# Eight of the sixteen difference chunks of a batch built by TensorE, and three hand-overs rewritten, in a two-layer graph kernel

## The reference

```python
def L0(x, adj, W, b, a):                      # 4 heads of 32 channels
    h = (x @ W + b).reshape(Bb, Nn, H, D)
    e = e_i[:, :, None, :] + e_j[:, None, :, :]         # e_i, e_j: h times the two halves of a
    e = where(adj > 0, where(e > 0, e, 0.2 * e), NEG)
    return einsum('bijh,bjhd->bihd', softmax(e, axis=2), h)

def L1(x, adj, W1, b1, g1, be1, W2, b2, Wg, ...):
    D = abs(x[:, :, None, :] - x[:, None, :, :])        # 32 x 256 x 256 x 128
    h = einsum('bijc,oc->bijo', D, W1) + b1             # 64 channels out
    m, v = mean(h, (0, 1, 2)), mean((h - m) ** 2, (0, 1, 2))
    h = leaky((h - m) / sqrt(v + EPS) * g1 + be1)
    A = softmax(where(adj > 0, h @ W2.T + b2, NEG), axis=-1)
    ...                                                 # y from A and x, normalised; [x, y] @ Wt.T + bt
x = layernorm(x + L0(x, adj, ...)); x = layernorm(x + L1(x, adj, ...))
```

## Time and profile before

| | us |
|---|---|
| median of 3 runs | 2476.84 |
| lowest, highest | 2466.27, 2483.92 |
| profiled execution | 2493.66 (span 2491.8) |

### The profile page before, as it was taken

How to read it: one execution, slowest core, us unless ns; L and a number is a source line. 1 busy time by engine, 2 the same in 40 slices (tenths; PEclk the granted TensorE clock), 3 DMA queues, 4 the chain that set the end, 5 groups by cost and what they waited for, 6 DMA issues and landing times.

```text
span 2491.8 us, 35885 instructions
## 1 busy us (share of the span) xinstructions
PE 2032.6 (82%) x12869; PEld 822.0 (33%) x12869; DVE 2112.6 (85%) x2600; ACT 2252.3 (90%) x3500; POOL 53.7 (2%) x50
## 2 busy tenths in 40 slices
PE   5777766888888888888888888887888888888876
PEld 3555542323333323233323232232222222222225
DVE  4888866999999999999999999999878888788866
ACT  4999977999999999999999999996989889899975
POOL 0000000000000000000000000000000000000000
PEclk8999977999999999999999999998989999899997
DMA  4111113444444444444444444445988889899872
GB/s 113 39 39 46 39 37 125 169 175 171 167 178 166 174 165 171 174 171 173 171 167 169 172 173 166 179 163 202 349 301 316 316 304 334 289 324 332 319 245 68
DMA packets 230503, 470.49 MB, mean 189 GB/s; under 512 B 53496, under 2 KB 144312, under 8 KB 213944
## 3 DMA queue, kind: packets, MB, share of 16 engines
q1 hardware_dynamic: 229264, 467.84, 51.3%
q10 hardware_dynamic: 1064, 0.36, 0.1%
HBM read 254.19 MB, written 213.91 MB: 188 GB/s over the span
## 4 chain that ended last, share of the span: by engine, by line
ACT 25%; PE 23%; issue 17%; DVE 15%; DMA 11%; SPq 7%; POOL 2%; ACTq 0%; POOLq 0%; DVEq 0%
PE banks L880 11%; ACT banks L635 11%; DMA ring_scores<-sring 6%; DVE diff L1242 6%; ACT hcopy L632 5%; ACT habs L632 5%; DMA ub<-ring_scores 5%; DVE ring L1095 4%; PE banks L791 2%; SPq L440 2%; POOL ub L500 2%; ACT diff L620 2%; SPq L420 2%; DVE diff L1256 2%; PE banks L895 2%
## 5 line engine op out<-in xcount | busy, mean ns | idle before, releaser
L880 PE MATMUL banks<-diff,w1t 128*64 128x512 f32 x5136 | 1228.6, 609 | 193.0 <-ACT banks L635 142.3
L1242 DVE TENSOR_TENSOR diff<-ring 128x2048 f32<-128x2048 f32 x352 | 802.9, 2289 | 116.6 <-PE banks L880 116.6
L880 PEld LDWEIGHTS banks<-diff,w1t 128*64 128x64 f32 x5136 | 344.7, 138 | 937.0 <-issue 855.6
L635 ACT ACTIVATE banks<-banks,par 128x1024 f32<-128x1024 f32 x512 | 559.4, 1093 | 7.1 <-PE banks L880 4.8
L1256 DVE TENSOR_SCALAR diff<-diff 128x2048 int32<-128x2048 int32 x354 | 415.6, 1220 | 0.0
L1370 DVE TENSOR_TENSOR diff<-ring 128x2048 f32<-128x2048 f32 x128 | 292.7, 2287 | 43.7 <-PE banks L880 43.7
L620 ACT ACTIVATE diff<-banks 128x2048 f32<-128x2048 f32 x128 | 240.3, 1878 | 12.6 <-PE banks L895 12.6
L632 ACT ACTIVATE hcopy<-banks 128x1024 f32<-128x1024 f32 x192 | 197.1, 1027 | 18.3 <-PE banks L880 18.1
L632 ACT ACTIVATE habs<-banks 128x1024 f32<-128x1024 f32 x192 | 197.0, 1026 | 18.4 <-PE banks L880 18.1
L895 PE MATMUL banks<-pick,yt 32*128 32x256 f32 x2560 | 185.0, 403 | 10.7 <-DMA yt<-xrows 10.7
L656 ACT ACTIVATE habs<-banks,par 128x1024 f32<-128x1024 f32 x128 | 153.5, 1199 | 43.5 <-PE banks L880 43.5
(11 more groups left out here) (216 smaller groups left out, 1886.4 us busy)
## 6 DMA issues: line engine op xcount, KB each, us to landing
diff<-kept_two SPq DMA_DIRECT2D x86, 1024.0 KB, 7.0
kept_two<-hcopy SPq DMA_DIRECT2D x128, 512.0 KB, 2.6
kept_two<-habs SPq DMA_DIRECT2D x128, 512.0 KB, 2.6
hcopy<-kept_two SPq DMA_DIRECT2D x42, 1024.0 KB, 7.2
kept_one<-hcopy SPq DMA_DIRECT2D x64, 512.0 KB, 2.6
kept_one<-habs SPq DMA_DIRECT2D x64, 512.0 KB, 2.6
hcopy<-kept_one SPq DMA_DIRECT2D x64, 512.0 KB, 7.4
habs<-kept_one SPq DMA_DIRECT2D x64, 512.0 KB, 7.8
```

Source lines behind the costliest of these rows:

```text
L635: nc.scalar.activation(h, h, ACT.Square, bias=par[:, 53:54], accum_out=column(SQUARES + c)).then_inc(sq_done, 1)
L880: last = nc.tensor.matmul(dst[half * O:(half + 1) * O, bank * BANK:(bank + 1) * BANK], w1t[:, :], src[:, m * BANK:(m + 1) * BANK], start=T ...
L1242: v.tensor_tensor(shaped(diff[:, c % ND, :]), xj, xi_, ALU.subtract).then_inc(sub_done, 1)
```

## The change

`ORDER` now lists four units of four chunks: (k,0), (4+k,0), (k,1), (4+k,1). All eight rectangles come from TensorE. ScalarE reads `dps` for the chunks (k,0), as before with their sum; VectorE reads it for the chunks (k,1), by a bit operation from PSUM to `diff` (`absolute_of_picked`). The picks stand behind the second and the fourth chunk of a unit; ScalarE's pass over `dps` stands behind the second. `diff` has five slots. In stage 2 VectorE alone normalises, in place in `rows`; TensorE transposes from `rows`, over four PSUM regions. The first group of rows is stored and waited for alone, then `xblk` of batch 0 is loaded, then the other 15 groups are stored. At the start, ScalarE's queue issues the small vectors ahead of the weights, and the sync queue issues the loads of `rows` once weights, vectors and `b0b` have landed.

```diff
-    ND = 4
+    ND = 5
     HC = CH // 2
     BLK = 16
 
-    ORDER = [(0, 0), (4, 0), (4, 1), (1, 0), (5, 0), (5, 1), (2, 0), (6, 0), (6, 1), (3, 0), (7, 0), (7, 1),
-             (0, 1), (1, 1), (2, 1), (3, 1)]
-    ON_PE = [(0, 0), (1, 0), (2, 0), (3, 0), (0, 1)]
+    ORDER = [(0, 0), (4, 0), (0, 1), (4, 1), (1, 0), (5, 0), (1, 1), (5, 1),
+             (2, 0), (6, 0), (2, 1), (6, 1), (3, 0), (7, 0), (3, 1), (7, 1)]
     REDONE = [(0, 0), (1, 0), (2, 0), (3, 0)]
-    NP, NR = len(ON_PE), len(REDONE)
+    NP, NR = 2 * RECTS, len(REDONE)
     NK = CHUNKS - NR
     KB = 8
-    PE_AT = [j for j, c in enumerate(ORDER) if c in ON_PE]
...
@@ -332,6 +322,9 @@
 
             load_l0(0, 0)
             load_l0(1, 1)
+            sp.wait_ge(w_loaded, 64)
+            sp.wait_ge(a_loaded, 48)
+            sp.wait_ge(b0b_loaded, 16)
             for g in range(4):
                 part = slice(g * TILES // 4, (g + 1) * TILES // 4)
                 sp.dma_start(rows[:, part, :], rows_in[:, part, :]).then_inc(rows_loaded, 16)
...
-            sp.wait_ge(rows_out, 16 * (TILES // 4))
+            def store_rows(g, done):
+
+                sp.wait_ge(ln_row, g + 1)
+                sp.dma_start(xrows[g * 4 * P:(g + 1) * 4 * P, :].rearrange("(t p) c -> p t c", p=P),
+                             rows[:, 4 * g:4 * g + 4, :]).then_inc(done, 16)
+
+            store_rows(0, rows_out_first)
+            sp.wait_ge(rows_out_first, 16)
             load_blocks_of_x(0)
+            for g in range(1, TILES // 4):
+                store_rows(g, rows_out)
             load_blocks_of_x(1)
+            sp.wait_ge(rows_out, 16 * (TILES // 4 - 1))
...
-            def norm_rows(g, q, first=False):
-
-                if not first:
-                    act.wait_ge(ln_tr, g - 1)
-                    act.wait_ge(ln_stored, g - 1)
...
-            act.wait_ge(ln_ready, 2)
-            norm_rows(0, 0, True)
-            norm_rows(1, 1, True)
-            to_ring(0, 0)
-            for g in range(2, TILES // 4 - 1, 2):
-                norm_rows(g, 0)
-                to_ring(g - 1, 1)
-                norm_rows(g + 1, 1)
-                to_ring(g, 0)
-            to_ring(TILES // 4 - 1, 1)
+            for g in range(TILES // 4):
+                to_ring(g, g % 4)
...
+            def absolute(b, q):
+
+                j = 4 * q
+                act.wait_ge(pd_ready, b * NP + 2 * q + 1)
+                if b or q:
                     act.wait_ge(h_ready, in_order(b, j) - ND + 1)
-                dst = diff[:, in_order(b, j) % ND, :]
-                if ORDER[j] in REDONE:
-                    nc.scalar.activation(dst, dps, ACT.Abs, accum_out=column(EVENS + b * NR + REDONE.index(ORDER[j]))).then_inc(abs_pe, 1)
-                else:
-                    nc.scalar.activation(dst, dps, ACT.Abs).then_inc(abs_pe, 1)
+                nc.scalar.activation(diff[:, in_order(b, j) % ND, :], dps, ACT.Abs,
+                                     accum_out=column(EVENS + b * NR + q)).then_inc(abs_even, 1)
...
             for b in range(B):
                 for j in range(CHUNKS):
                     sum_h(b, j)
-                    if j + 3 in PE_AT:
-                        absolute(b, j + 3)
-                    if j + 3 == CHUNKS and b + 1 < B:
+                    if j % 4 == 1 and j + 3 < CHUNKS:
+                        absolute(b, (j + 3) // 4)
+                    elif j % 4 == 1 and b + 1 < B:
                         absolute(b + 1, 0)
...
-            def transpose_rows(g, q, first=False):
+            def transpose_rows(g, q):
                 pe.wait_ge(ln_row, g + 1)
-                pe.wait_ge(ln_row_act, g + 1)
-                if not first:
-                    pe.wait_ge(ln_copied, g - 1)
+                if g >= 4:
+                    pe.wait_ge(ln_copied, g - 3)
                 for t in range(4):
-                    last = nc.tensor.transpose(ps[q][:, t * P:(t + 1) * P], onorm[q][:, t * P:(t + 1) * P], ident[:, :])
+                    last = nc.tensor.transpose(ps[q][:, t * P:(t + 1) * P], rows[:, 4 * g + t, :], ident[:, :])
                 last.then_inc(ln_tr, 1)
-            transpose_rows(0, 0, True)
-            transpose_rows(1, 1, True)
-            for g in range(2, TILES // 4 - 1, 2):
-                transpose_rows(g, 0)
-                transpose_rows(g + 1, 1)
+
+            for g in range(TILES // 4):
+                transpose_rows(g, g % 4)
             pe.wait_ge(ln_copied, TILES // 4)
...
+            def pick_differences(b, r):
+
+                k, tp = ORDER[2 * r]
+                if r == 0:
                     pe.wait_ge(blk_loaded[b % 2], 256 * (b // 2 + 1))
-                if n:
-                    pe.wait_ge(abs_pe, n)
-                e = 2 * pe_before(j)
+                if r % 2:
+                    pe.wait_ge(abs_even, b * RECTS + r // 2 + 1)
+                elif b or r:
+                    pe.wait_ge(abs_odd, b * RECTS + r // 2)
+                e = 2 * (RECTS * tp + k)
...
             pick_differences(0, 0)
             pe.wait_ge(shift_sum, 1)
             nc.tensor.matmul(ps[3][:, 0:1], agg[:, 1, :], par[:, 52:53], start=True, stop=True).then_inc(shift_half, 1)
+            pick_differences(0, 1)
             pe.wait_ge(shift_ready, 1)
             for b in range(B):
                 for j in range(CHUNKS):
-                    if j in PE_AT:
-                        stat_chunk(in_order(b, j), True, b * NP + pe_before(j) + 1)
+                    if j % 4 == 0:
+                        pe.wait_ge(abs_even, b * RECTS + j // 4 + 1)
+                    elif j % 4 == 2:
+                        pe.wait_ge(abs_odd, b * RECTS + j // 4 + 1)
                     else:
-                        stat_chunk(in_order(b, j), False, b * (CHUNKS - NP) + dve_before(j) + 1)
-                    if j + 3 in PE_AT:
-                        pick_differences(b, j + 3)
-                    if j + 3 == CHUNKS and b + 1 < B:
-                        pick_differences(b + 1, 0)
+                        pe.wait_ge(abs_dve, b * PAIRS + j // 2 + 1)
+                    stat_chunk(in_order(b, j))
+                    if j % 2 and j + 3 < CHUNKS:
+                        pick_differences(b, (j + 3) // 2)
+                    elif j % 2 and b + 1 < B:
+                        pick_differences(b + 1, (j + 3 - CHUNKS) // 2)
...
+            def norm_rows(g):
+
+                for t in range(4):
+                    tile = rows[:, 4 * g + t, :]
+                    last = v.tensor_scalar(tile, tile, bass.AP(mu, g * 4 + t, [[TILES, P], [1, 1]]),
                                            bass.AP(rstd, g * 4 + t, [[TILES, P], [1, 1]]), ALU.subtract, ALU.mult)
                 last.then_inc(ln_row, 1)
...
+            for g in range(TILES // 4):
+                norm_rows(g)
             dve.wait_ge(ln_copied, TILES // 4)
             dve.wait_ge(ln_tr, TILES // 4)
-            dve.wait_ge(ln_stored, TILES // 4)
...
+            def absolute_of_picked(b, q):
+
+                j = 4 * q + 2
+                dve.wait_ge(pd_ready, b * NP + 2 * q + 2)
+                if b or q:
+                    dve.wait_ge(h_ready, in_order(b, j) - ND + 1)
+                v.tensor_scalar(diff[:, in_order(b, j) % ND, :].bitcast(I32), dps.bitcast(I32), ABS_BITS, None,
+                                ALU.bitwise_and).then_inc(abs_odd, 1)
...
+                for q in range(RECTS):
+                    z = b * PAIRS + 2 * q + 1
+                    subtract(b, 4 * q + 1)
+                    subtract(b, 4 * q + 3)
+                    absolute(in_order(b, 4 * q + 1), z)
+                    if b == 0 and q == 0:
+                        dve.wait_ge(abs_even, 1)
+                        v.tensor_scalar(par[:, 52:53], yt[:, SUMS + EVENS:SUMS + EVENS + 1], -1.0 / CH, None,
+                                        ALU.mult).then_inc(shift_sum, 1)
+                        dve.wait_ge(shift_half, 1)
+                        v.tensor_copy(par[:, 53:54], ps[3][:, 0:1]).then_inc(shift_ready, 1)
+                    absolute_of_picked(b, q)
+                    absolute(in_order(b, 4 * q + 3), z + 1)
```

More of the change, by code:

```diff
@@ L308, in kept_before @@
             return sum(c not in REDONE for c in ORDER[:j])
-        def pe_before(j):
-            return sum(a < j for a in PE_AT)
-        def dve_before(j):
-            return j - pe_before(j)
         block = ctx.enter_context(nc.Block())
@@ L351, in _ @@
                 load_l0(b + 1, 1)
-            for g in range(TILES // 4):
-                sp.wait_ge(ln_stored, g + 1)
-                sp.dma_start(xrows[g * 4 * P:(g + 1) * 4 * P, :].rearrange("(t p) c -> p t c", p=P),
-                             rows[:, 4 * g:4 * g + 4, :]).then_inc(rows_out, 16)
             def load_blocks_of_x(b):
@@ L507, in _ @@
         def _(act):
+            for k in range(2):
+                act.dma_start(acols[:, k:k + 1],
+                              bass.AP(a0.tensor, a0.offset + k * DH, [[0, H], [1, DH], [1, 1]])).then_inc(a_loaded, 16)
```

(1 more changed line is left out.)

72 lines of the change are left out of this document (8 added, 64 removed).

## The result

| | median us | lowest, highest | runs |
|---|---|---|---|
| before | 2476.65 | 2456.09, 2500.14 | 14 |
| changed | 2490.7 | 2468.9, 2503.76 | 14 |

The ratio is 1.0069, with a 95% interval of 1.0036 to 1.0102: within the 1% or so that the prediction counts as no change, though the interval leaves out 1, so in these runs the changed kernel was a little slower. (Executions more than 1.5% above the fastest of the same kernel are a slow state and are left out of the ratios and of the medians of before that the experiments give, 2 of 30 and 7 of 13 runs of it.) The profiled execution of the changed kernel took 2475.71 us (span 2473.8), that of before 2493.66. The two profiles alone would say "18 us faster", the medians say 14 us slower; the size of the change has to be read stage by stage.

A forecast was written before the change was run, and what follows sets the result against it. It took a loop between ScalarE and TensorE through two PSUM projection buffers as the bound. Pass +21.9, hand-over -12.6, start -2.9 give +6.4 us, put on the median: 2483 us, range 2455 to 2515 (8 in 10).

The forecast's parts named there:

- the sum: Whole kernel: steady pass +21.9, hand-over -12.6 and start -2.9 give +6.4 us; end of pass counted zero.
- The loop through two engines: Statistics pass: two PSUM projection buffers force 3.33 us between ScalarE starts two chunks apart; unit 10.37 us, batch 41.48.
- ScalarE's wait: Statistics pass: ScalarE idles about 1.1 us ahead of a copy once a unit, some 140 us in all.
- The start: Kernel start: VectorE's first step 6.8 us earlier, of which 2.9 us are left at batch 2; bounds 0 and 6.8.
- Carried through to its end: Layer 0: what is left of the start's gain at batch 2, 2.9 us, lasts to the layer's end.
- The hand-over: Row normalisation into the statistics pass: steady pass starts at 393.5 instead of 406.1, gaining 12.6 us; bounds 8 and 16.
- End of the pass: Last batch of the statistics pass: loses its pass over dps in both kernels; counted zero, bounds -2 and +2 us.
- The PSUM pass: VectorE's new read of dps from PSUM in the statistics pass: 2.3 us, bounds 1.2 and 2.72.
- The fifth slot gives nothing by itself: Statistics pass: the fifth diff slot only removes VectorE waits that were not on the path, so no gain.
- Rival (a): Statistics pass: idle time goes unpaid, engine work sets the pass, TensorE longest at 9.30 us; 2346 us in all; chance 0.12.
- Rival (b): Statistics pass: VectorE's read of dps slows ScalarE by 0.46 us a unit, 59 us in all; 2542 us; chance 0.18.
- Rival (c): Statistics pass: VectorE is the bound, needing a PSUM pass of 3.6 us; chance included in (b)'s 0.18.

The follow-up runs named there:

- experiment 3: The changed kernel, unchanged, run once more beside 30 runs of the kernel before: 2486.54 us, ratio 0.9996.
- experiment 2: Two kernels against the kernel before: rewritten start, row normalisation and first store alone, 2468.43 us; new statistics pass alone, 2516.72 us.
- experiment 4: The changed kernel with an added ScalarE copy, never read, before each of 128 lone squares: 2490.85 us, ratio 1.0006 to the kernel before.
- experiment 6: The changed kernel with ScalarE's dps pass behind the lone square, TensorE's picks earlier, VectorE's sign pass ahead of its second subtract: 2375.0 us, ratio 0.9537.
- experiment 5: The changed kernel with four diff slots instead of five: 2507.71 us, ratio 1.0077 to the kernel before.
- experiment 7: The kernel of experiment 6 without VectorE's reordering, both subtracts again ahead of the first sign pass: 2498.86 us, ratio 1.0071 to the kernel before.
- experiment 9: The kernel of experiment 6 with four diff slots instead of five: 2961.27 us, ratio 1.1941 to the kernel before.
- experiment 8: The kernel before with ScalarE's pass over dps one chunk later in its stream: 2808.2 us, ratio 1.1339.

## Why the prediction was right, and where its terms were not

It said 2483 us, +0.3%; the medians gave 2490.7 in the session of the result (before: 2476.65) and 2486.54 in experiment 3 (before: 2487.45). To the end of the pass the sum was +6.4 us, measured +3.1 in the profiles and +1.9 between the kernels that end there. That it came so near is in part luck: the loss in the pass was 2.7 us larger than said and the gain ahead of it 5.1 us larger, and these errors go against each other. The total alone proves little, as a change that neither gained nor cost anything would have come out at "the same" too; experiment 2 shows that both terms are there.

- **The loop through two engines: right.** Unit 10.37 said, 10.39 read; batch 41.48 and 41.56. That it is the loop and not an engine's work is shown by both directions: more work on ScalarE costs next to nothing (experiment 4), and the same work in another order, with ScalarE's pass behind the lone square and the moves on TensorE and VectorE that go with it, takes 109 us less (experiment 6). That it is the loop of these two engines and not VectorE's is shown by the chain of waits, which leaves VectorE out here and takes it in with four slots (experiment 5). Over 32 batches +24.6 us (41.56 - 40.79, times 32), where +21.9 was said: 0.02 us a unit over 128 units.
- **ScalarE's wait:** said 1.1 us and some 140 in all; read 0.90 and 109.2 in the window, about 115 over 128 units. The rows hold the rest: the lone square starts 1.26 us after the square ahead of it, not 1.10, and the next copy 2.10 after that, not 1.10, which is 1.16 us of idle time; the bracket counts it only from the end of the short row that reads the sum.
- **The start:** 2.9 us said, 5.1 read at the first row tile. The step that was off: the four loads of `rows` were given the 15.71 us of queue that they took before; issued alone they took 10.13, so batch 2's x stood at TensorE at 33.05 and not at 36.8, and nearly the whole of the upper bound of 6.8 came. "Carried through to its end" was wrong too: of the 6.67 us at batch 2, 1.6 were gone at the first row tile; where they went isn't shown.
- **The hand-over:** 12.6 said. The steady pass counted back from 387.58 by 2.10 starts at 385.5, against 406.1, 20.6 earlier; less 5.1 from the start, 15.5 from the hand-over, inside the bounds of 8 to 16. The largest part of the excess is the second chunk, whose copy followed the first square by 1.71 us (385.87, 387.58) and not by 3.5: of the sixteen records at 382.23, 5.31 us in all, the first projection took the slow 3.6 and the second only the 1.7 of the full clock. The first pick took 1.15 us where 2.09, that of before, had been set; VectorE was free of the tiles as computed (16.48 us for 64, said 16.3). The experiment with the hand-overs alone gives 21.5 for both.
- **End of the pass:** counted zero; what is left of the sum is 3.1 - 24.6 + 20.6 = -0.9.
- **The PSUM pass:** 2.3 said, 2.284 read. VectorE's unit is idle 1.43 us as said ("over 1 us").
- **"The fifth slot gives nothing by itself": wrong.** The step that failed took VectorE's waits for a slot as off the path, because three chunks in the kernel before take 7.29 us without them, and carried that over to the changed kernel. It doesn't hold for the whole batch even before: the chain that gave the batch its 40.79 us goes through VectorE's two subtracts, which wait for a slot, and VectorE has 13.6% of the chain in the pass. Once a batch TensorE waits for the sign pass behind such subtracts, and ScalarE then waits 1.13 us for TensorE (kernel before, 440 to 1697 us):

```profile
PE banks L880 <- DVE diff L1256: 41.8, 30, 1.4
ACT habs L632 <- PE banks L880: 16.9, 15, 1.1
ACT hcopy L632 <- PE banks L880: 16.9, 15, 1.1
```

  In the changed kernel the slot keeps VectorE's second subtract early enough for the loop of TensorE and ScalarE to stay the longest; with four, VectorE's own ring is 0.11 us a unit longer (14.4 us over 128), and in the moved order, whose unit is shorter, 4.48 us (573.8 over 128). A fifth slot in the kernel before was not tried.

**Rival (a)**, engine work sets the pass, is refuted for this kernel by experiment 4 and by the 98 us and more that each engine stands idle in the pass. Its bound is real, though: with the order of experiment 6 TensorE is the longest, with 9.55 us a unit where 9.30 was computed from the rows. The Trainium skill (Perfetto Trace Analysis, Identifying the Most-Contended Engine) would have the engine with the highest occupancy optimised first. Here that was ScalarE. It was given 5% less work and the pass took 24 us longer; given 128 us more, it took 0.6 us longer. So the measurement goes against the rule for this pass. **Rival (b)**, VectorE's PSUM read slows ScalarE, is refuted: the mean copy is 1.033 us against 1.027, 0.02 a unit in all, which is about what the unit was off by. The copy and square that run beside VectorE's pass (913.17 and 914.16) take 1.05 and 1.12 us; those at the same place before, without it (934.18 and 935.17), took 1.04 and 1.12. **Rival (c)** fell with 2.284 us in this order; with four slots, or in the order of experiment 7, VectorE's ring is the bound all the same, by its waits and not by a pass of 3.6 us.

**What stays open:** why the stage behind the pass, with the same code, takes from 738.5 us (span 2463.0 in experiment 3) to 769.7 us (span 2960.0 in experiment 9) from execution to execution. In the eleven profiled executions that have it, it has the same 3936 matmul records; the shortest had a granted clock of 0.95 in it and the two longest 0.92, while TensorE's busy time differed by 20 of the 31 us. So the clock goes with most of the spread, without being shown to be its cause. The spread is larger than the change.

## What to carry to other kernels

Before you count an engine's work, look for the loop: buffers between two engines set a least time from one release to the use of what it released (here 3.33 us for two PSUM buffers), and each place in the order has to put that much work between them; an order that does, with the same work, was worth 109 us. When you move one stream, move what waits behind it on each other engine too, and count slots again: VectorE's part of the move or the fifth slot, left out, took back all of it and more. Where a stage that was not touched spreads by more than the change, cut it off and time the rest.

## What the runs showed of the hardware that was not expected

- The time of an execution goes with its mean granted clock. Over the 14 runs of the changed kernel the clock was 0.961 (2503.76 us) to 0.973 (2468.9 us), correlation -0.92, about 25 us for 0.01; over the 12 of experiment 3, -0.88. The kernels without the scores pass had 0.971 to 0.972 and 0.980 to 0.982, and the runs of each agreed within 2.3 us. Which is cause and which effect is not shown.
- Where TensorE waited 2.45 us and more again and again, the granted clock of the pass was 0.90 (experiment 8) and 0.86 (experiment 9); with waits of 0.62 us (changed kernel) and 1.00 us (experiment 7) a unit, and up to 1.7 us once a batch (the kernel before), it was 1.00. The waits' length and TensorE's share of work changed together, so neither is singled out.
- The same bit operation on 128x2048 values takes 1.22 us from SBUF and 2.284 us from PSUM.
